# Attention on one core: key splitting, moments and maxima row move to GpSimd and ScalarE, the causal mask of the maximum pass moves to TensorE

## The reference, cut to what matters

```python
x = x + _layernorm(_L0_attn_ref(_layernorm(x), W_attn, b_attn, W_proj, b_proj))
# inside _L0_attn_ref, after q and k are turned by an angle that depends on the head:
att = jnp.einsum('bhqd,bhkd->bhqk', q, k) * (1.0 / math.sqrt(hd))
att = jnp.where(causal, att, -jnp.inf)
y = jnp.einsum('bhqk,bhkd->bhqd', softmax(att), v)
```

## Time and profile before

| | us |
|---|---|
| median of 3 runs | 3547.5 (3546.36 to 3552.07) |
| profiled execution, its own time | 3569.08 |
| its span, first to last instruction | 3567.4 |
| PE busy in the span | 2933.1 (82%) |
| DVE busy | 2072.3 (58%) |
| ACT busy | 1260.0 (35%) |
| POOL busy | 545.8 (15%) |

### The profile page before, as it was taken

How to read it: one execution, slowest core, us unless ns; L and a number is a source line. 1 busy time by engine, 2 the same in 40 slices (tenths; PEclk the granted TensorE clock), 3 DMA queues, 4 the chain that set the end, 5 groups by cost and what they waited for, 6 DMA issues and landing times. The chain is left out here.

```text
span 3567.4 us, 44916 instructions
## 1 busy us (share of the span) xinstructions
PE 2933.1 (82%) x15561; PEld 1781.8 (50%) x15561; DVE 2072.3 (58%) x5935; ACT 1260.0 (35%) x2085; POOL 545.8 (15%) x701
## 2 busy tenths in 40 slices
PE   3899898989898989943788886489998989999876
PEld 1334343434344444322667775455665656566554
DVE  3777777767676867755466655444525344353442
ACT  1455555555455555631221221013132231313211
POOL 3000202020202020110111211001202012020211
PEclk8899899999999999976888897789999999999998
DMA  4141414132332423131222221200101011010000
GB/s 132 51 126 44 149 43 136 56 112 80 100 92 78 115 72 108 32 110 49 90 89 84 92 97 60 90 12 27 51 0 50 12 38 50 0 50 6 18 24 12
DMA packets 172172, 235.43 MB, mean 66 GB/s; under 512 B 17117, under 2 KB 138873, under 8 KB 165762
## 3 DMA queue, kind: packets, MB, share of 16 engines
q1 hardware_dynamic: 172002, 233.27, 21.3%
HBM read 131.74 MB, written 101.50 MB: 65 GB/s over the span
## 5 line engine op out<-in xcount | busy, mean ns | idle before, releaser
L939 ACT ACTIVATE pt<-ps 128x1024 f32<-128x1024 f32 (+3 forms) x768 | 601.7, 812 | 478.8 <-PE ps L854 331.5
L739 DVE CUSTOM_DVE_ANT_0 masked<-ps,mask_q 128x128 bf16<-128x128 f32 (+3 forms) x1024 | 473.1, 484 | 157.2 <-PE ps L832 152.3
L832 PE MATMUL ps<-sk,sq 96*128 96x512 bf16 (+3 forms) x1536 | 453.2, 349 | 122.2 <-DVE mx L743 47.4
L851 PE MATMUL ps<-sq,sk 99*128 99x512 bf16 (+3 forms) x1536 | 421.9, 343 | 17.4 <-DMA sq<-scratch_nm_parts 13.4
L743 DVE TENSOR_REDUCE mx<-ps 128x1 f32<-128x512 f32 x512 | 350.7, 685 | 97.1 <-PE ps L832 96.5
L832 PEld LDWEIGHTS ps<-sk,sq 96*128 96x128 bf16 x1536 | 138.7, 99 | 472.1 <-issue 147.1
L870 PE MATMUL ps<-pt,val 128*32 128x512 f32 (+3 forms) x3072 | 342.8, 520 | 0.7 <-ACT yt L947 0.6
L1940 PE MATMUL ps<-eht,w_fc 128*128 128x512 f32 x512 | 252.5, 641 | 9.4 <-ACT eht L1991 9.4
L1952 PE MATMUL ps<-w_fc,eyb 128*128 128x256 f32 x1024 | 228.7, 381 | 15.1 <-ACT eyb L1999 15.1
L851 PEld LDWEIGHTS ps<-sq,sk 99*128 99x128 bf16 x1536 | 153.5, 101 | 162.0 <-issue 43.0
L1952 PEld LDWEIGHTS ps<-w_fc,eyb 128*128 128x128 f32 x1024 | 193.2, 190 | 53.3 <-ACT eyb L1999 24.1
(11 more groups left out here) (288 smaller groups left out, 4828.1 us busy)
## 6 DMA issues: line engine op xcount, KB each, us to landing
scratch_stacks<-part SPq DMA_DIRECT2D x32, 768.0 KB, 3.6
sq<-scratch_stacks SPq DMA_DIRECT2D x32, 768.0 KB, 8.0
sk<-scratch_stacks SPq DMA_DIRECT2D x32, 768.0 KB, 9.4
scratch_stacks<-part SPq DMA_DIRECT2D x32, 512.0 KB, 4.5
x<-in_L_attn_x SPq DMA_DIRECT2D x8, 1024.0 KB, 13.6
scratch_stacks<-part SPq DMA_DIRECT2D x32, 256.0 KB, 4.9
xr<-in_L_attn_x SPq DMA_DIRECT2D x8, 1024.0 KB, 6.1
scratch_x<-xr SPq DMA_DIRECT2D x8, 1024.0 KB, 10.2
```

The source lines that it names most:

```text
L739: nc.vector.tensor_tensor_reduce(mem["masked"][:, slot, 0:n], ps[:, RING[slot], 0:n], mem["mask_q"][:, BANK - n:BANK], 1.0, -3e38, ALU.add ...
L832: nc.tensor.matmul(ps[:, bank, 0:n], sq[0:ROWS, h, i * P:(i + 1) * P], sk[0:ROWS, h, half * BANK:half * BANK + n], start=True, stop=True)\
L851: last = nc.tensor.matmul(ps[:, bank, 0:n], sk[0:ROWS_M, h, j * P:(j + 1) * P], sq[0:ROWS_M, h, q0:q0 + n], start=True, stop=not diag)
L939: nc.scalar.activation(pt[:, u % 3, 2 * pair:2 * pair + 2, 0:n], ps[:, bank:bank + 2, 0:n], ACT.Exp, scale=SCALE).then_inc(e["exp_done"], 1)
```

## The change

- The k halves of `parts` move from DVE to POOL, behind the q halves, in the same order of steps.
- `rows` is cut in two. A new step `nmax` (unit 8, 20, 32, 44) is DVE's fold alone. `rows` and its DMA step `nm` move one unit later. PE's transpose is as before, ACT copies the row out of PSUM, and POOL does the four splitting instructions.
- `bn_aggr` and its drain are gone from DVE. The short chain on POOL reads the raw statistics and becomes ten instructions.
- In the `max` pass, PE adds the mask with an identity matmul of 128 columns after each of the 1024 diagonal matmuls, and DVE does a plain maximum everywhere.

```diff
@@ attention_steps
-                put(at + 8, ("rows", b, s), ("nm", b, s))
+                put(at + 8, ("nmax", b, s))
+                put(at + 9, ("rows", b, s), ("nm", b, s))
@@ rstd_and_shift
-    nc.gpsimd.tensor_scalar(tmp, moments[:, :, 1], EPS_LN, None, ALU.add).then_inc(ready, 1)
-    nc.gpsimd.tensor_scalar(shift, moments[:, :, 0], -1.0, None, ALU.mult).then_inc(ready, 1)
+    g.tensor_tensor(diff, stats[:, :, 1], stats[:, :, 4], ALU.subtract).then_inc(ready, 1)
+    g.tensor_tensor(sums, stats[:, :, 1], stats[:, :, 4], ALU.add).then_inc(ready, 1)
+    g.tensor_tensor(spread_, stats[:, :, 2], stats[:, :, 5], ALU.add).then_inc(ready, 1)
+    g.tensor_tensor(square, diff, diff, ALU.mult).then_inc(ready, 1)
+    g.tensor_scalar(spread_, spread_, 1.0 / C, EPS_LN, ALU.mult, ALU.add).then_inc(ready, 1)
+    g.tensor_scalar(square, square, 0.25, None, ALU.mult).then_inc(ready, 1)
+    g.tensor_scalar(shift, sums, -0.5, None, ALU.mult).then_inc(ready, 1)
+    g.tensor_tensor(square, square, spread_, ALU.add).then_inc(ready, 1)
     (with waits between them; then the power and the product, as before)
@@ gpsimd
-                if kind == "parts" and a[0] == 0:
+                if kind == "parts":
+                elif kind == "rows":
+                    until_taken(g, step)
+                    nc.gpsimd.tensor_copy(nmp[:, 0, :], nmr[:, :])
+                    nc.gpsimd.tensor_tensor(nmr[:, :], nmr[:, :], nmp[:, 0, :], ALU.subtract)
+                    nc.gpsimd.tensor_copy(nmp[:, 1, :], nmr[:, :])
+                    nc.gpsimd.tensor_tensor(nmp[:, 2, :], nmr[:, :], nmp[:, 1, :], ALU.subtract)
@@ vector
-                        nc.vector.tensor_tensor_reduce(mem["masked"][:, slot, 0:n], ps[:, RING[slot], 0:n],
-                                                       mem["mask_q"][:, BANK - n:BANK], 1.0, -3e38, ALU.add, ALU.max,
-                                                       accum_out=mx[:, hh, i, half:half + 1]).then_inc(taken[slot], 1)
+                    nc.vector.reduce_max(mx[:, hh, i, half:half + 1], ps[:, RING[slot], 0:n], AX.X)\
+                        .then_inc(taken[slot], 1)
@@ tensor
+                    if diag:
+                        last = nc.tensor.matmul(ps[:, bank, n - P:n], w["ident16"][:, :], w["mask_qk"][:, :],
+                                                start=False, stop=True)
@@ scalar
+                elif kind == "rows":
+                    nc.scalar.copy(nmr[:, :], ps[0:R, RING[slot], 0:P]).then_inc(taken[slot], 1)
```

More of the change, by code:

```diff
@@ L515, in attention_steps @@
     order += [("stack", 0, s) for s in range(SETS - 1)] + [("v", 0, 0, n) for n in range(NHALF)]
-    order += [("max", 0, 0, n) for n in range(len(MU))] + [("rows", 0, 0), ("nm", 0, 0)]
+    order += [("max", 0, 0, n) for n in range(len(MU))] + [("nmax", 0, 0), ("rows", 0, 0), ("nm", 0, 0)]
     order += [("max", 0, 1, n) for n in range(EARLY)]
@@ L546, in rstd_of, with rstd_and_shift @@
     return nc.gpsimd.tensor_tensor(out, tmp, w["mhalf"][:, 0:n], ALU.pow)
[L549 to L557 removed]
+MOMENT_STEPS = 9
+def rstd_and_shift(nc, stats, rstd, shift, w, mom, ready, count):
+    diff, sums, spread_, square = (mom[:, n, :] for n in range(4))
+    g = nc.gpsimd
+    g.tensor_tensor(diff, stats[:, :, 1], stats[:, :, 4], ALU.subtract).then_inc(ready, 1)
+    g.tensor_tensor(sums, stats[:, :, 1], stats[:, :, 4], ALU.add).then_inc(ready, 1)
+    g.tensor_tensor(spread_, stats[:, :, 2], stats[:, :, 5], ALU.add).then_inc(ready, 1)
+    g.wait_ge(ready, count + 1)
+    g.tensor_tensor(square, diff, diff, ALU.mult).then_inc(ready, 1)
+    g.wait_ge(ready, count + 3)
+    g.tensor_scalar(spread_, spread_, 1.0 / C, EPS_LN, ALU.mult, ALU.add).then_inc(ready, 1)
+    g.wait_ge(ready, count + 4)
+    g.tensor_scalar(square, square, 0.25, None, ALU.mult).then_inc(ready, 1)
+    g.tensor_scalar(shift, sums, -0.5, None, ALU.mult).then_inc(ready, 1)
+    g.wait_ge(ready, count + 7)
+    g.tensor_tensor(square, square, spread_, ALU.add).then_inc(ready, 1)
+    g.wait_ge(ready, count + 8)
+    g.tensor_tensor(rstd, square, w["mhalf"][:, 0:NT], ALU.pow).then_inc(ready, 1)
+    g.wait_ge(ready, count + 9)
+    return g.tensor_tensor(shift, shift, rstd, ALU.mult)
 def attention_loop(nc, io, w, ps):
@@ L694, in _ @@
                     until_taken(g, ("qk", b, r, chunk, n))
-                    done = halves_before(b, *a)
+                    done = nth[step]
                     if chunk:
@@ L737, in _ @@
                     v.wait_ge(filled[slot], uses + 1)
-                    if (i * P) // BANK == half:
-                        nc.vector.tensor_tensor_reduce(mem["masked"][:, slot, 0:n], ps[:, RING[slot], 0:n],
-                                                       mem["mask_q"][:, BANK - n:BANK], 1.0, -3e38, ALU.add, ALU.max,
-                                                       accum_out=mx[:, hh, i, half:half + 1]).then_inc(taken[slot], 1)
[L742 to L745, removed]
+                    nc.vector.reduce_max(mx[:, hh, i, half:half + 1], ps[:, RING[slot], 0:n], AX.X)\
+                        .then_inc(taken[slot], 1)
+                elif kind == "nmax":
+                    if nth[step]:
+                        until_filled(v, ("rows", *divmod(nth[step] - 1, SETS)))
                     nc.vector.drain()
@@ L831, in _ @@
                         pe.wait_ge(e["stack_in"][s], 32 * (b + 1))
-                    nc.tensor.matmul(ps[:, bank, 0:n], sq[0:ROWS, h, i * P:(i + 1) * P],
-                                     sk[0:ROWS, h, half * BANK:half * BANK + n], start=True, stop=True)\
-                        .then_inc(filled[slot], 1)
+                    diag = (i * P) // BANK == half
+                    last = nc.tensor.matmul(ps[:, bank, 0:n], sq[0:ROWS, h, i * P:(i + 1) * P],
+                                            sk[0:ROWS, h, half * BANK:half * BANK + n], start=True, stop=not diag)
+                    if diag:
+                        last = nc.tensor.matmul(ps[:, bank, n - P:n], w["ident16"][:, :], w["mask_qk"][:, :],
+                                                start=False, stop=True)
+                    last.then_inc(filled[slot], 1)
                 elif kind == "rows":
```

83 lines of the change are left out of this document (33 added, 50 removed).

## The result

The changed kernel takes 3534.5 us (median of 6 runs, 3529.83 to 3538.12), the kernel before on the same chip 3546.9 (6 runs). The ratio is 0.9963, 95% interval 0.9950 to 0.9975: faster by 0.37%, where I forecast slower by 0.3%. The time lies inside the range, on the other side of no change. The profiled execution's own time is 3536.93, its span 3535.2.

A forecast was written before the change was run, and what follows sets the result against it. PE was nearest the bound, in a mixture with waits for DVE and low clock after gaps. Six turns at +1.0 us, batch 0 -5.6, batch 7 +4 and the start +6 gave +10.4 on 3547.5: 3558 us, range 3525 to 3590.

The forecast's parts named there:

- The waits moved to POOL's queue: Main forecast: waits shift from DVE to POOL's queue, 3558 us, own range 3545 to 3575, chance 0.38.
- Units 9 to 12 grow by 5.7 us: Unit 9: the short chain queues behind the row on POOL, ACT waits 5.3 us, PE stands about 5.
- Units 33 to 36 grow by 2.4: Unit 34: chain starts behind unit 33's row, ACT waits about 4 us; less the former 1.79 us row wait.
- 7 times each, 57 us: The 5.7 and 2.4 us waits per turn, which go if POOL's order costs nothing, giving 3501 us.
- The rival that would have these waits vanish: Row and short chain finish before ACT gets there, DVE's relief decides: 3501 us; chance 0.30, milder results included.
- milder form: Half of that rival: 4 us less waiting in both places and smaller ring waits, 3530 us; within its 0.30 chance.
- Units 19 to 24: POOL's queue and the DMAs hold unit 24 until 19.6 us after unit 19, against 21.2: 1.6 us gained.
- Row and k halves off DVE: Units 8, 32, 44 get back 2.6, 0.7, 0.7 us; k halves give 4.5 us in units 24 to 33.
- I charge about 5 us per batch: Mask matmuls on PE, 1024 at 0.055 us: 59 us if fully paid, 7.4 per batch, charged about 5.
- The start: Ahead of the first `exp`: eight halves run one after the other on POOL, 6 us later.
- Moments: `bn_aggr` with its drain leaves DVE, 24 times per batch at 0.25 us, mostly inside other waits: 1.5 us gained.
- 0.32: Chance given to the changed kernel being faster; slower by over 0.2% had 0.50, within 0.2% had 0.18.

The follow-up runs named there:

- y2: Changed kernel with POOL alone walking the short chain of x_norm and xn1 ahead of the last row: 3473.3 us, ratio 0.9788 to the kernel before.
- y3: y2 with the k halves of the first chunk two units later, behind the adds and row of unit 21: 3448.3 us, ratio 0.9719 to the kernel before.
- x2: Changed kernel with the k halves of `parts` back on DVE: 3557.5 us, ratio 1.0024 to the kernel before.
- x3: Changed kernel with the whole row step (fold, copy, splitting) back on DVE in its old unit: 3475.3 us, ratio 0.9775 to the kernel before.
- x1: Changed kernel with the masks of the maximum pass back in DVE's custom instruction: 3522.9 us, ratio 0.9925 to the kernel before.
- y1: Kernel before with only the masks moved to PE and plain maxima on DVE: 3571.2 us, ratio 1.0059 to the kernel before.
- y4: y3 with the masks taken back from PE to DVE: 3429.0 us, ratio 0.9665 to the kernel before.
- w1: Changed kernel with every mask matmul issued twice: 3569.7 us, ratio 1.0049 to the kernel before.
- w3: Kernel before run once more, unedited, for a second trace: 3562.6 us, a single execution.
- w4: Changed kernel run once more, unedited, for a second trace: 3545.8 us, a single execution.
- x4: Changed kernel with `bn_aggr` back on DVE and the short chain of four instructions: 3527.5 us, ratio 0.9923 to the kernel before.
- w2: y4 with the moments' aggregation back on DVE: 3448.9 us, ratio 0.9696 to the kernel before.

## Why the prediction went wrong, point by point

**The waits moved to POOL's queue: right, in place and size.** "Units 9 to 12 grow by 5.7 us": +5.6 (10.55 to 16.15). "Units 33 to 36 grow by 2.4": +2.2. That "7 times each, 57 us" would come back if POOL's order cost nothing was put to the test by y2, which changes that order alone, and got 62. The unknown step prices were good: the row 1.6 us (1.7 forecast), ACT's copy 0.25 (0.3), the chain 3.8 (4.3). The rival that would have these waits vanish is refuted as to its mechanism; the time ended on its side, near the 3530 of its milder form, for other reasons.

**Units 19 to 24: right as a stretch.** I had unit 24 no sooner than 19.6 us after unit 19, by POOL's queue. Timeline of POOL, SP and PE of the kernel after, unit 19 starting at 721.76:
```profile
724.05 1.41 POOL L748 TENSOR_TENSOR xr<-xr,att 128x256 f32<-128x256 f32 x2 [6.40 <-ACT att L955]
725.41 0.61 POOL L713 CAST part<-qk 128x512 bf16<-128x512 f32 x1
726.10 1.17 POOL L715 TENSOR_TENSOR qk<-qk,part 128x512 f32<-128x512 f32 x1
...
735.57 0.28 POOL L727 CAST nmp<-nmr 32x128 bf16<-32x128 f32 x1
...
737.21 0.33 SPq L687 DMA_DIRECT2D scratch_nm_parts<-nmp  x1
...
740.97 0.61 PE L850 MATMUL ps<-sq,sk 99*128 99x512 bf16 x1 [4.89 <-DMA sq<-scratch_nm_parts]
```
Adds, half, adds, half, adds, row, then the DMAs: unit 24 starts 19.2 us after unit 19, and PE stands 4.89 us for it. y3 takes one k half and its followers out of that chain and unit 24 starts 3.7 us sooner. Set against x2 the k halves by themselves make this stretch 1.0 us longer. The subtraction on POOL takes 1.17 us against DVE's 0.69, 1.7 times as much. The Trainium skill (GPSIMD Engine Reference, section 4.1, Engine selection) says about twice; the measured ratio is somewhat below that.

**Row and k halves off DVE: right for the change as a whole, too high for each part.** Unit 8 got back 2.8 us, with 2.6 forecast; units 32 and 44 0.75 each (0.7); unit 21 2.6 and unit 29 3.0 (unit means of the first two traces, batches 1 to 6). But with the rest of the change in place, the row alone is worth 1.5 us in unit 8 and 0.7 in units 20, 32 and 44 (x3), and the k halves alone 1.9 us in units 24 to 33, where I had 4.5 (x2). The k halves as a whole are worth 22 us by x2, nearly half of it in batch 0's turn.

**The failed step: "I charge about 5 us per batch" for the masks.** The start-to-start price of one was right. Three neighbours in PE's timeline of the kernel after, at full clock:
```profile
1433.80 0.22 PE L831 MATMUL ps<-w_mask_qk,w_ident 128*128 128x128 bf16 x1
1433.86 0.22 PE L828 MATMUL ps<-sk,sq 96*128 96x128 bf16 x1
1433.91 0.22 PE L831 MATMUL ps<-w_mask_qk,w_ident 128*128 128x128 bf16 x1
```
What was wrong is the share that lies on the path. I took two thirds (39 of 59 us); three comparisons give 13 (x1), 21 (y1) and 19 us (y4 against y3), a quarter to over a third. By stretch, x1 against the changed kernel agrees with my charges in units 9 to 19 (1.2 us for 1.1) and 24 to 33 (1.3 for 1.4), but gives 0.4 us in units 0 to 9 where I charged 1.0, nothing in 36 to 48 where I charged 1.5, and -0.4 in 33 to 36. I had reasoned that a stretch with PE at 97% has no cover.

Where the cover lies is seen in the attention stage as a whole. Windows from the first `exp` to the last unit, of x1 (no mask on PE), w1 (two sets), y4 (none) and y1 (one set, else the kernel before):
```profile
120.20:1491.40 1371.20, 1250.20 (x8491) 583.89 (x8491) 880.35 (x2941) 788.64 (x1198) 348.44 (x614) 0.95 0.30 90
```
```profile
117.60:1544.30 1426.70, 1337.07 (x10461) 709.15 (x10459) 882.40 (x1957) 792.66 (x1198) 347.51 (x614) 0.96 0.29 86
```
```profile
117.40:1392.90 1275.50, 1213.11 (x8491) 569.58 (x8491) 878.46 (x2941) 786.34 (x1198) 347.52 (x614) 0.99 0.33 97
```
```profile
115.00:1532.90 1417.90, 1299.73 (x9478) 639.43 (x9476) 1015.78 (x2392) 789.15 (x1167) 195.47 (x252) 0.96 0.29 87
```
PE is busy for 1250 us and idle for 121 with no set, busy for 1293 and idle for 102 with one (mean of both traces of the changed kernel), and busy for 1337 and idle for 90 with two. So the first set adds 43 us of busy time and takes 19 out of the idle time, 23 us in net; the second adds 44 and takes only 12, 32 in net. y3 against y4 repeats the first step (41 more busy, 18 less idle), and y1 against the two traces of the kernel before has 39 and 25. Part of what hid the first set was used up by the second. Why busy time grows by some 43 us and not by 56 is not shown.

The idle time that is taken is made of small pieces: PE's weight loads wait for maxima, also in quiet units, and those waits shrink when PE arrives later. The waits of 116 to 1525 us, first of x1 (no mask on PE; the maximum has two lines there), then of w1 (two sets); one set stands above with 82.0:
```profile
PEld ps L836 <- DVE mx L769: 84.4, 160, 0.9
...
PEld ps L836 <- DVE mx L773: 61.3, 133, 1.0
```
```profile
PEld ps L828 <- DVE mx L765: 57.0, 121, 0.8
```
They go from 146 to 82 to 57 us. The first set took 64 us out of these waits and the second 25, more than left PE's idle time (19 and 12), so not all of this waiting had stopped a matmul; the direction is the same. The masks buy nothing on DVE, as forecast. Groups by form of the plain maximum, kernel after: busy, mean ns of one, idle before:
```profile
L765 DVE TENSOR_REDUCE mx<-ps 128x1 f32<-128x512 f32 x768 | 511.4, 684 | 192.5 <-PE ps L828 153.5 <-PE ps L831 35.9
...
L765 DVE TENSOR_REDUCE mx<-ps 128x1 f32<-128x128 f32 x256 | 72.4, 283 | 158.3 <-PE ps L831 158.3
```
684 and 283 ns, where the masked form took 0.69 and 0.28 us. So this part of the change costs in every setting tried.

**The start: "+6", measured +2.5.** Timeline of POOL and SP of the kernel after:
```profile
44.09 0.61 POOL L713 CAST part<-qk 128x512 bf16<-128x512 f32 x1 [9.62 <-ACT qk L977]
...
72.55 1.15 POOL L720 TENSOR_TENSOR part<-qk,part 128x512 bf16<-128x512 f32 x1
...
75.74 1.26 SPq L682 DMA_DIRECT2D sq<-scratch_stacks  x1
```
The eighth half ends at 73.7, not at 77.9. Of these 4.2 us, 1.7 are my error: the eight run without a gap, 3.7 us each. I let the second chunk of k wait the 9.0 us for the parts' DMA again; here POOL goes from the q halves to the k halves without waiting, so that DMA has landed by then. The other 2.5 us are an earlier begin (44.09 against 46.62) that is no effect of the change: the repetitions w3 and w4 begin at 45.49 and 45.77. Counted from the first half to the first `exp`, the change costs 3.6 us (69.5 before, 73.1 after, means of two traces).

**Moments: right, but never added up.** I counted the ten-instruction chain into ACT's waits (4.3 us in place of 2.6, twice a turn in seven turns, +24) and the aggregation into DVE's relief ("1.5 us" a turn, -12), and did not compare the two with each other. My own terms make this part of the change a loss of 12 us; x4 measures 14, and w2, without the waits, a relief of 11 to 20.

**The sum again.** With the masks at 18 us (the mean of the three) in place of 39, the prediction's own sum gives 3558 - 21 = 3537, and with the start at 2.5 in place of 6, 3533.5, beside 3534.5 measured. The masks alone turn the sign. That the numbers meet so closely is luck: the small misses of the other terms cancel, the traces of the stage would put the masks at 14 to 23 us, and of the 12.5 us between the medians the stretches explain only 7. The forecast was a small difference between large terms. By single experiments in the changed kernel, the row's new place costs 67 us in balance, the moments 14 and the masks 13, and the k halves gain 22. That is a loss of 72 where the whole gains 12, so such parts don't add up: they share waits. For the same reason the masks are not the only term that its own experiment contradicts: my terms give the row a cost of 25 us (57 for the two waits, 32 gained in units 8, 32 and 44) where x3 has 67, and the k halves a gain of about 37 (6.1 us in each of six turns, 6 in batch 0, less 6 at the start) where x2 has 22. These two errors point away from the measured sign and don't show in the stretches, whose misses add up to -2.4 us a turn; the masks' overcharge is 2.5. A sign that hangs on +10 us with one term of 39 us known to a factor of two deserved a chance near one half, not 0.32.

**What stays open.** How the gain splits among the parts, when they are undone one by one and share waits, is not settled. The attention stage and what is ahead of it account for -7 us by two traces of each kernel, while the medians differ by 12.5 us (8.9 to 17.7 by the interval). In the traces the untouched stages add another -17 us, at a granted clock 0.01 lower before the change. The unprofiled runs of the kernel before spread from 3538 to 3563 us on one chip, with the mean granted clock of the whole execution at 0.907 to 0.915, mostly the lower the longer the run, and have no trace. Whether it gets the lower clock in these stages more often than the changed one, and why, is not settled; the profiled executions of the kernel before lay 22 and 7 us above its medians.

## What to carry to other kernels

When work moves to an idle engine, ask first behind what it will stand in that engine's queue, and who waits for its neighbours: putting ten small instructions ahead of four, on an engine that is 25% busy, was worth 62 us of 3534, by the same two stretches that make up most of what the row's new place cost. Price a small added instruction by undoing it alone, and not by the busy share of its engine: of mask matmuls on an engine busy 93% of its stage, a quarter to over a third was paid, and of a second set about half. The best version has k halves and row on POOL with the short chain ahead and the first k halves two units later, and the masks on DVE: 3429 us.

## What the runs showed of the hardware

Windows of the attention stage, from the first `exp` to the last unit, of the kernel after, y2 and y3 in this order:
```profile
117.40:1509.50 1392.10, 1290.45 (x9475) 643.08 (x9475) 876.22 (x1957) 791.04 (x1198) 347.63 (x614) 0.96 0.30 88
```
```profile
117.80:1445.30 1327.50, 1264.27 (x9476) 631.85 (x9477) 873.86 (x1957) 789.69 (x1198) 348.31 (x614) 0.98 0.31 93
```
```profile
119.90:1418.60 1298.70, 1254.47 (x9475) 627.40 (x9475) 873.20 (x1956) 788.87 (x1198) 347.75 (x614) 0.99 0.32 95
```
The same matmuls keep PE busy for 1290, 1264 and 1254 us, as the mean granted clock rises from 0.96 to 0.99. The time at half clock in the stage is 111, 49 and 17 us. It vanishes with the waits, and no work was taken away from any engine. PE's idle time (the window less PE's busy time) falls from 102 to 63 and 44 us; beside that PE's busy time for the same matmuls falls by 26 and 36 us. Each microsecond that PE's idle time fell went with 1.7 us of the stage from the kernel after to y2, and with 1.5 from y2 to y3.

The cost of POOL's small instructions falls much less than their size: 0.17 to 0.3 us start to start on 128x8, 0.36 for a cast and 0.48 for a subtraction on 32x128, 0.69 and 1.22 on 128x512; the power on 128x8 alone takes 1.67. On DVE the maximum with the mask added takes as long as the plain one, 684 ns on 512 columns and 283 on 128.
